# fp16 parts of x, q and k split with tokens in the partitions and turned by transposing DMAs, in an attention and FFN block on one core

## What is computed

```python
def ref(x, Wq, Wkv, Wout, bout, w_gate, w_up, w_down):
    xn = layernorm(x)
    # attention, 16 heads of 16; k and v are the same matrix
    q, kv = rotary(xn @ Wq), rotary(xn @ Wkv)
    att = softmax(q * 16 ** -0.5 @ kv.T)          # per head
    a = (att @ kv) @ Wout + bout
    # FFN, integer weights times 1/127, 768 hidden
    h = silu(xn @ wg.T) * (xn @ wu.T)
    return x + a + h @ wd.T
```

## Time and profile before

| | us |
|---|---|
| median of 3 runs | 850.45 |
| the profiled execution | 852.67 |
| its span | 850.9 |
| busy: TensorE, VectorE, ScalarE, GpSimd | 819.2, 758.6, 687.8, 213.3 |
| granted TensorE clock, mean over the span | 0.996 |

### The profile page before, as it was taken

The page is one execution under the profiler, slowest core; times in us unless marked ns, Lnnn a source line. Parts: engine busy times, 40 slices in busy tenths (PEclk is TensorE's granted clock), DMA queues, the critical chain, the costliest instruction groups (busy, mean ns, idle before and its releaser), DMA issues.

```text
span 850.9 us, 19487 instructions
## 1 busy us (share of the span) xinstructions
PE 819.2 (96%) x7500; PEld 316.0 (37%) x7500; DVE 758.6 (89%) x937; ACT 687.8 (81%) x1275; POOL 213.3 (25%) x458
## 2 busy tenths in 40 slices
PE   4898999999999999999999999999999999999997
PEld 2455555565433333333333333333333333333234
DVE  5897788888799999999999999999999999999802
ACT  4555354443699999999999999999999999999982
POOL 3623354334302100000222222222222222222210
PEclk9999999999999999999999999999999999999999
DMA  9212100111211111111221222122212121122222
GB/s 300 73 50 78 60 25 28 49 50 53 64 28 34 31 29 33 45 29 33 52 54 48 54 55 59 48 49 58 54 50 55 52 60 50 50 56 56 80 65 80
DMA packets 63615, 48.49 MB, mean 57 GB/s; under 512 B 23308, under 2 KB 53836, under 8 KB 63524
## 3 DMA queue, kind: packets, MB, share of 16 engines
q1 hardware_dynamic: 63524, 47.26, 20.0%
HBM read 28.57 MB, written 16.90 MB: 53 GB/s over the span
## 4 chain that ended last, share of the span: by engine, by line
PE 89%; ACT 3%; DVE 3%; issue 2%; POOL 0%; DVEq 0%; ACTq 0%
PE ps L740 33%; PE ps L757 18%; PE ps L722 14%; PE ps L600 8%; PE ps L628 4%; ACT arena L994 3%; PE ps L577 1%; PE ps L579 1%; PE ps L578 1%; PE ps L617 1%; PE ps L660 1%; PE ps L768 1%; PE ps L552 1%; DVE side L1094 1%; PE ps L784 1%
## 5 line engine op out<-in xcount | busy, mean ns | idle before, releaser
L1153 DVE TENSOR_REDUCE negmax<-ps 128x2 f32<-128x1024 f32 x512 | 588.9, 1211 | 8.6 <-PE ps L757 6.4
L994 ACT ACTIVATE arena<-ps 128x512 f32<-128x512 f32 x1024 | 555.5, 595 | 32.2 <-PE ps L722 10.5
L740 PE MATMUL ps<-arena 128*32 128x256 f32 x4072 | 326.5, 392 | 2.4 <-issue 2.2
L722 PE MATMUL ps<-qs,ks 51*128 51x512 f16 x1024 | 197.9, 382 | 3.4 <-ACT arena L994 2.2
L757 PE MATMUL ps<-ks,qs 48*128 48x512 f16 x972 | 189.4, 386 | 0.0
L740 PEld LDWEIGHTS ps<-arena 128*32 128x32 f32 x4072 | 80.4, 107 | 128.1 <-issue 127.0
L757 PEld LDWEIGHTS ps<-ks,qs 48*128 48x128 f16 x972 | 46.5, 92 | 195.1 <-DVE negmax L1153 136.1
L924 ACT ACTIVATE side<-ps 128x512 f32<-128x512 f32 x48 | 28.6, 597 | 90.6 <-PE ps L600 90.1
L600 PE MATMUL ps<-arena,side 128*128 128x512 f16 x384 | 91.3, 386 | 1.1 <-DVE side L1094 1.0
L722 PEld LDWEIGHTS ps<-qs,ks 51*128 51x128 f16 x1024 | 50.7, 93 | 78.1 <-ACT arena L994 46.1
L1399 POOL TENSOR_TENSOR arena<-arena,x_all 128x256 f32<-128x256 f32 x22 | 16.1, 732 | 229.6 <-ACT arena L1015 229.6
(11 more groups left out here) (116 smaller groups left out, 558.8 us busy)
## 6 DMA issues: line engine op xcount, KB each, us to landing
parts_d<-arena SPq DMA_DIRECT2D x64, 128.0 KB
x_all<-x_dram SPq DMA_DIRECT2D x8, 512.0 KB, 9.3
qs<-parts_d SPq DMA_DIRECT2D x64, 64.0 KB, 1.9
ks<-parts_d SPq DMA_DIRECT2D x64, 64.0 KB, 1.9
o_d<-arena SPq DMA_DIRECT2D x124, 32.0 KB
arena<-o_d SPq DMA_DIRECT2D x24, 128.0 KB
arena<-inv_d SPq DMA_DIRECT2D x48, 64.0 KB
out_dram<-arena SPq DMA_DIRECT2D x24, 128.0 KB, 1.8
```

Source lines behind the costliest of these rows:

```text
L722: mm = pe.matmul(ps[:, score_bank(place(p, kt, 2 * half + a)), :], ks[ring][top:top + ROWS, kt * P:(kt + 1) * P], qs[ring][top:top + ROWS, ...
L740: mm = pe.matmul(ps[32 * j:32 * j + 32, 7, cols], vstage[pl % 2][:, j % 2, kt, :], probs[PER_STEP * (kt % PBUF) + j][:, cols], start=(kt = ...
L994: act.activation(probs[PER_STEP * (kt % PBUF) + j], ps[:, score_bank(place(p, kt, j)), :], ACT.Exp).then_inc(exp_done, 1)
L1153: dve.tensor_reduce(negmax[pl % 2][:, h, :, kt], ps[:, bank:bank + 2, :], AX.X, ALU.max, negate=True).then_inc(max_done, 1)
```

## The change

What is split and turned, and by whom:

- x (chunks 1 to 7): ScalarE writes the high part `x_hi` from `xn` in SBUF, all 1024 columns in one operation; VectorE the low part `x_lo` = `xn` - `x_hi`, also in one, ahead of the first reduce of the chunk. Both have tokens in the partitions. SP turns each into `xh` and `xl` with one transposing DMA of 8 blocks. Chunk 0 is turned as before.
- q and k (all chunks): ScalarE writes `qk_hi` from `qk` in SBUF per token tile, ahead of the chunk's own silu; GpSimd writes `qk_lo` per token tile (`low_qk`, four subtractions of 512 columns, ahead of `keep_values`; in chunk 0 between its low parts of the hidden values). SP turns each with one transposing DMA of 16 blocks, waits until both have landed, and stores as before.
- TensorE has no `turn_x` (but chunk 0's) and no `turn_qk`; the waits on their banks go. The last chunk's down waits for the hidden values' parts alone.
- SP's order is, per chunk: turn x of c + 1, turn q and k of c, store c. The pair loads stand behind the second chunk's stores as before, the turn of the row maxima ahead of the last chunk's turns.
- VectorE: no `low_qk`; `low_w` moved between products 3 and 4 and behind 4 of chunk 0; twelve moments behind chunk 0's last product; `inverse` moved into `rope_chunk`.
- ScalarE waits for the last chunk's turns ahead of the first exponential, as the new tiles lie where the probabilities go.

The core of the diff:

```diff
@@ sync @@
 def store_chunk(b, s):
     c = b * CPB + s
+    sp.wait_ge(qk_turned, 32 * (c + 1))
     for g in range(4):
-        sp.wait_ge(lo_done, 4 * c + g + 1)
         for k in range(NPART):
             ...
+def turn_qk(c):
+    if c:
+        for g in range(4):
+            sp.wait_ge(parts_stored[g], 16 * NPART * c)
+    sp.wait_ge(qk_hi_done, CT * (c + 1))
+    sp.dma_start_transpose(parts[:, 0, :, :].rearrange("p g (t n) -> p (g t) n", t=CT),
+                           qk_hi.rearrange("p g t n -> p (g t n)")).then_inc(qk_turned, 16)
+    sp.wait_ge(qk_lo_done, CT * (c + 1))
+    sp.dma_start_transpose(parts[:, 1, :, :].rearrange("p g (t n) -> p (g t) n", t=CT),
+                           qk_lo.rearrange("p g t n -> p (g t n)")).then_inc(qk_turned, 16)
+def turn_x(c):
+    if c >= 2:
+        sp.wait_ge(up_done, KH * (c - 1))
+    sp.wait_ge(x_hi_done, c)
+    sp.dma_start_transpose(xh[c % 2].rearrange("p k (t n) -> p (k t) n", t=CT),
+                           x_hi.rearrange("p k t n -> p (k t n)")).then_inc(x_turned, 16)
+    sp.wait_ge(x_lo_done, c)
+    sp.dma_start_transpose(xl[c % 2].rearrange("p k (t n) -> p (k t) n", t=CT),
+                           x_lo.rearrange("p k t n -> p (k t n)")).then_inc(x_turned, 16)
...
@@ tensor @@
 def project(c):
-    pe.wait_ge(xT_copied, x_copies(c, KD - 1))
     if c:
-        pe.wait_ge(xl_ready, KD * (c + 1))
+        pe.wait_ge(x_turned, 32 * c)
+    else:
+        pe.wait_ge(xT_copied, 2 * KD)
...
     gate_up(c, 0)
     gate_up(c, 1)
-    if c + 1 < NCHUNK:
-        turn_x(c + 1)
...
-    if units[UNITS:]:
-        lead(units[UNITS])
-    turn_qk(c)
-    for n in units[UNITS + 1:]:
+    for n in units[UNITS:]:
         lead(n)
@@ scalar @@
 for c in range(NCHUNK):
     more = c + 1 < NCHUNK
-    if c:
-        high_qk(c - 1)
     if more:
         normalise(c + 1)
+        high_x(c + 1)
+    if c:
+        high_qk(c)
     silu(c, 0)
     silu(c, 1)
+    if c == 0:
+        high_qk(0)
     high(c, 0)
-    if more:
-        copy_x(c + 1, 0)
-        if c:
-            copy_x(c + 1, 1)
@@ vector @@
+def low_x(c):
+    if c == 1:
+        dve.wait_ge(wud_ready, 1)
+    else:
+        dve.wait_ge(x_turned, 32 * (c - 1))
+    dve.wait_ge(x_hi_done, c)
+    dve.tensor_tensor(x_lo.rearrange("p k t n -> p t k n"), xn.rearrange("p t (k n) -> p t k n", k=KD),
+                      x_hi.rearrange("p k t n -> p t k n"), ALU.subtract).then_inc(x_lo_done, 1)
...
     for j in range(2, KH):
         if c + 1 < NCHUNK and j == 2:
-            low_x(c + 1, 0)
+            low_x(c + 1)
...
@@ gpsimd @@
+def low_qk(c, t):
+    ...
+    pool.wait_ge(qk_hi_done, CT * c + t + 1)
+    pool.tensor_tensor(qk_lo[:, :, t, :], qk[:, t, :].rearrange("p (g n) -> p g n", g=4), qk_hi[:, :, t, :],
+                       ALU.subtract).then_inc(qk_lo_done, 1)
```

More of the change, by code:

```diff
@@ L160, in build @@
         front_room = used[0]
-        parts = [carve(NPART * CHUNK // 2, FP16, "p (s n) -> p s n", s=NPART) for _ in range(4)]
+        parts = carve(4 * NPART * CHUNK // 2, FP16, "p (s g n) -> p s g n", s=NPART, g=4)
         atile_hi = [carve(HG * P // 2, FP16, "p (g n) -> p g n", g=HG) for _ in range(2)]
@@ L462, in _ @@
                     sp.dma_start(ks[i][top:top + MPARTS, :], unit_rows[:, :]).then_inc(units_in, 16)
[L463 to L468, removed]
+            for c in range(NCHUNK):
+                if c + 1 < NCHUNK:
+                    turn_x(c + 1)
+                else:
                     turn_rows(0, 0)
                     load_mrows(0, 0)
+                turn_qk(c)
                 store_chunk(c // CPB, c % CPB)
+                if c + 1 == CPB:
+                    for p in range(2):
+                        load_pair(p, p)
             def load_last(g, landed):
@@ L603, in gate_up @@
                     mm.then_inc(done, 1)
[L605 to L618, removed]
             def down(c, t):
@@ L932, in high_qk @@
             def high_qk(c):
[L933 to L938, removed]
+                if c:
+                    act.wait_ge(qk_turned, 32 * c)
+                for t in range(CT):
+                    act.wait_ge(rope_done, CT * c + t + 1)
+                    act.activation(qk_hi[:, :, t, :], qk[:, t, :].rearrange("p (g n) -> p g n", g=4), ACT.Copy
+                                   ).then_inc(qk_hi_done, 1)
             roots(0, CT)
@@ L1067, in rotated @@
                 if t == 0:
[L1068 removed]
+                    dve.wait_ge(qk_hi_done, CT * c)
+                    dve.wait_ge(qk_lo_done, CT * c)
                     dve.wait_ge(v_kept, c)
@@ L1095, in gated @@
                                          ALU.mult, ALU.mult).then_inc(hid_done, 1)
-            def low_qk(c):
-                for g in range(4):
-                    dve.wait_ge(hi_done, 4 * c + g + 1)
-                    dve.tensor_tensor(parts[g][:, 1, :], bank_turn(g), parts[g][:, 0, :], ALU.subtract
-                                      ).then_inc(lo_done, 1)
             def add_ffn(c, t):
@@ L1115, in rope_chunk @@
                         rotated(c, t - 1)
+                    if c in (1, 2) and t == 1:
+                        inverse(c + 1, 2 * CT + 3 * CT * (c - 1), 2 * CT + 3 * CT * c)
                 rotated(c, CT - 1)
@@ L1352, in _ @@
                     split_max(0, 0)
+                if c:
+                    for t in range(CT):
+                        low_qk(c, t)
                 keep_values(c)
@@ L1355, in _ @@
                     low_hid(c, j)
+                    if c == 0 and 1 <= j <= CT:
+                        low_qk(0, j - 1)
             def stage_values(p, batch, slot, pair):
```

140 lines of the change are left out of this document (73 added, 67 removed).

## The result

The changed kernel takes 841.1 us (median of 4 runs, 840.25 to 842.6) where the kernel before, on the same chip, takes 849.88: ratio 0.9894, interval 0.9871 to 0.9917. The steps of the forecast added up to 1.2 us less; 8 to 9 came.

The account below looks back on a forecast made before the run. The prediction took TensorE as the bound, with VectorE second by tenths of a microsecond. Terms of -2.0 (chunks 0 to 2), +2.3 (chunks 3 to 6) and -1.5 (chunk 7) summed to -1.2 us: 849.3 us, no difference, range 842 to 864.

Parts of the forecast that it names:

- Removed from TensorE, steady chunks: Chunks 3 to 6: 2.6 us of turns leave TensorE per chunk, yet chunks grow 0.55 to 0.6, +2.3 us in all.
- The 2.6 us are gone twice over: Steady chunks: TensorE waits 2 us for the first reduce and 1 us at the end for silu and product.
- The transposing DMAs: SP queue: each further block costs 0.18 us, so turns hold SP 2.4 us (x) and 3.8 us (q and k).
- the idle TensorE ahead of it grows from 2.7 us to about 4.5: Chunk 2: TensorE's wait ahead of the first lead matmul lengthens, that matmul coming at 82.6 us.
- I keep that loss: Chunk 2: the stretch of lower clock (0.72 of full in 80 to 92 us) was assumed to remain.
- partly fill gaps: Chunk 0: weights' low parts moved between products on VectorE partly fill gaps; products end at 37.1, -2.5 us.
- I leave 1.1 of the 2.5: Chunk 1: of chunk 0's 2.5 us gain 1.1 stays; low x ready at 56.4, chunk 2 starts at 64.3.
- ScalarE's copies stay equal in number of columns: ScalarE's splitting copies, with GpSimd's new subtractions, were costed at nothing.
- Chunk 7: Last chunk: down no longer waits for low parts and starts right behind the last lead, -1.5 us.
- A: Rival: SP becomes the bound if a block costs over 0.33 us; 862 us at 0.37, 967 at 0.72; chance 0.15.
- C: Rival: TensorE's waits in chunks 3 to 6 lower its clock, +13.6 us, 863 us; chance 0.1.
- B: Rival: low x cheaper or not locked out, 846.3 us; wholly covered, chunks of 23.8 and 842 us; chance 0.2.

Follow-up runs that it names:

- e6: Changed kernel with TensorE turning the identity matrix, unread, where it had turned x and q and k: 845.15 us, ratio 0.9942.
- e2: Changed kernel with the next chunk's low part of x made among the rotations (chunk 1: ahead of the first gated product): 834.41 us, ratio 0.9826.
- e5: The kernel before, unchanged, profiled a second time: 848.19 us.
- e1: Changed kernel with SP's first pair loads held back until the first gate group of chunk 2 is done: 844.92 us, ratio 0.9951.
- e7: Changed kernel with each transposing DMA cut in two, 8 and 4 blocks instead of 16 and 8: 842.53 us, ratio 0.9907.
- e8: Changed kernel with the low parts of q and k on VectorE instead of GpSimd, both inputs in SBUF: 849.77 us, ratio 0.9999.
- e4: Changed kernel with weights' low parts, moments and inverses put back where the kernel before has them: 847.01 us, ratio 0.9974.
- e9: Changed kernel with low part of x among the rotations and, in chunks 2 to 6, lead pairs and reduces one place later: 833.17 us, ratio 0.9798.
- e10: Changed kernel with the low part of x among the rotations, run again for comparison on one chip: 835.04 us, ratio 0.9820.
- e11: The changed kernel again, unchanged, for comparison on one chip: 841.52 us, ratio 0.9903.

## Why the prediction was wrong

**Removed from TensorE, steady chunks: right in mechanism.** "The 2.6 us are gone twice over" holds: the rows in chunk 4 name the low part of x, the reduce and the last product, e6 gives the turns back for 0.65 us, and e2 shows what paces the chunks. The size was off: +0.1 to +0.2 in each of chunks 3, 4 and 6 where +0.55 stood. The wait of "0.73" was 0.69; the operation itself took 1.21 instead of 1.27 and low x ended 0.2 us sooner, and the handovers behind it took 8.7 us instead of 8.85. In chunk 5 the forecast added 0.6 to a period of 25.86, but that chunk's extra 0.7 came from the collision in the earlier trace rows, and the collision is gone: `combine` never took over 178 ns in the changed kernel. Together 2.4 of the missing 5.9 us.

**The transposing DMAs: the mis-sized term that cost most.** "A turn of x holds SP 2.4 us, one of q and k 3.8": measured 1.2 and 1.8 to 2.3. With it the sum from low x to the end of the stores, 16.2 us in the forecast, was 13.1 (54.17 to 67.27). The other half is the start of that sum: low x at 56.4 forecast, 54.1 measured. Of the 3.1 us the hold alone gave 4.5: the three transposes ahead of the stores took 5.6 us of SP, gaps included, where 10.1 stood. The landing took 1.5 back, 2.7 us from the end of the last one's hold to the first store (59.76 to 62.42) where 1.2 stood. So stores ended 5.3 us before the forecast's 72.6, and "first lead 82.6" became 76.08. It could not have come earlier: it is TensorE's own arrival. The step that failed is "the idle TensorE ahead of it grows from 2.7 us to about 4.5"; it vanished, and "I keep that loss" of the clock did not hold in the profiled execution either. Chunk 2 became 24.6 us long, against 27.5 in e5 and 31.4 in the execution that the forecast worked from, of which it took off 0.9. e1 puts the idle time back and pays 3.3 us at the next mark.

**Chunk 0: -2.5 forecast, -3.8 measured.** VectorE, the kernel before again (e5), then the changed one:

```profile
35.11 0.69 DVE L1094 SCALAR_TENSOR_TENSOR side<-ps,side 128x512 f32<-128x512 f32 x1 [0.67 <-ACT side L924]
35.72 2.94 DVE L1086 SCALAR_TENSOR_TENSOR arena<-wqkv,wgain,arena 128x512 f16<-128x512 f32 x2
```
```profile
31.73 1.06 DVE L1113 SCALAR_TENSOR_TENSOR arena<-wqkv,wgain,arena 128x512 f16<-128x512 f32 x1
32.85 0.69 DVE L1121 SCALAR_TENSOR_TENSOR side<-ps,side 128x512 f32<-128x512 f32 x1
33.46 0.90 DVE L1113 SCALAR_TENSOR_TENSOR arena<-wqkv,wgain,arena 128x512 f16<-128x512 f32 x1
34.58 0.69 DVE L1121 SCALAR_TENSOR_TENSOR side<-ps,side 128x512 f32<-128x512 f32 x1 [0.21 <-PE ps L626]
```

The low parts "partly fill gaps" was too timid: at their new place they take 1.96 us instead of 2.94 and none of it is on the path, because six moments that stood there (2 x 1.26) had moved behind the last product, under the projection. The projection starts at 35.41 against 39.19. (In chunk 0 single executions stray: the 35.41 of the changed kernel is 36.64 in e7, with 1.2 us of it older than anything that e7 changes.)

**Chunk 1: "I leave 1.1 of the 2.5".** 2.65 of 3.8 were left. The moments cost what they should (35.18 to 39.99, 4.8 us ahead of the rotation), against 5.8 in e5 (38.58 to 44.36: six moments, the inverse with its wait for ScalarE, low q and k). And low x, made whole, no longer stands between the fourth and fifth product: 0.6 us more. What took the rest back is a term that the forecast put at nothing ("ScalarE's copies stay equal in number of columns"): their place. VectorE's rotations start 4.4 us earlier than in e5, but the chunk's first silu starts at 50.81 against 50.67. ScalarE now has ahead of it the norm (at 44.19, behind the moved `inverse`), the high part of x and those of q and k of this same chunk, until 49.49, and then a table load of 1.28 us, which in e5 lay at 45.35. TensorE waits for the products behind that silu:

```profile
52.27 3.61 PE L626 MATMUL ps<-arena,side 128*128 128x512 f16 x16 [2.33 <-DVE side L1121]
```

No run moves these copies, so what they cost is read from the rows and not tested.

**Chunk 7: right.** -1.45 for -1.5, and the wait it names is gone: the last lead starts at 212.54 after 1.65 us for its reduce, down at 212.93.

**The rivals.** A (SP the bound) is out: at most 0.11 us a block, by the longest hold (1.91 us for 8), where 0.33 were needed, and e7. C (the clock) is out in the steady chunks: waits of 1.64 and 0.93 us left it at full in every profiled execution. B's number is the nearest to the result (842), but its mechanism is not what the changed kernel did: low x was locked out and uncovered. e2 covers it, and there B's figure of 23.8 for covered chunks was right (23.6).

The Trainium skill's rule on the pair of ports (SBUF — State Buffer, SBUF: two separate sides) is borne out in both directions: VectorE, the later one at 126.75, takes 0.69 us longer beside GpSimd's first (from 126.42, 1.16 long alone, so until 127.58, 0.83 us behind VectorE's start), and GpSimd's second then waits for VectorE (3.24 us for its two, 2.31 where nothing is beside them). That is a lock for a whole instruction, and in e8, where VectorE came first, VectorE waited for nothing. Its entry of 1309 ns for a 128x128 by DMA (VectorE: DVE Perf Modes, The three transpose paths) is near SP's time for a DMA of one block (1.14 us) and of eight (1.23 at the least), and does not multiply with the blocks.

What stays open: the execution of before with the low clock is explained as far as its longer wait (2.72 against 1.30 us) goes, but not why its loads took 1.6 us longer to release the lead matmul. Nor is it known what of the difference of the medians is the clock's.

## What to carry to other kernels

A DMA's hold on the queue and its transfer are two terms; price them apart, and when both bounds of one are far apart, run the sum at each and look for a wait that vanishes at one end: there the outcome jumps. A load issued early in a pipeline can be worth more than the engine time that the change is about: holding it back cost 3.3 us here, the 2.6 us of turns given back to TensorE 0.65 a steady chunk. One profiled execution can hold a stretch of low clock that the next does not; look at a second before a stage is priced. When the work that covered a late engine is taken away, find what was late behind it, and move that too: here 1.7 us in each steady chunk waited for one line's place.

## What the runs showed of the hardware

- Transposing DMAs, SBUF to SBUF, fp16 blocks of 128x128: SP held 1.14 us for 1 block (the median), and at the least 1.19 for 4, 1.23 for 8, 1.32 for 16 (2.26 to 2.58 for one right behind another of 16); landing after 2.3, 2.4, 3.2 and 4.4 us at the least.
- Low parts on VectorE, float32 less fp16, both in SBUF: 1024 columns 1.21 us, four of 512 columns 3.33, or 0.83 each, against 0.62 each from PSUM (four in 2.48).
- The granted clock fell to its lower level, half of full, in stretches of 3.4 us (6.8 once). In the front of the thirteen profiled executions, from some 17 us on, where the record of the clock begins, it did so nine times, each time just behind an idle TensorE: 2.02 us idle (e4, at 66.6), 2.08 (e9), 2.33 (e7), 2.55 (e1), 2.72 (before), 2.73 (e10), 3.05 and 3.99 (e8), 4.08 (e4). The same idle times also left it at full: 2.33 in the changed kernel, e1 and e11, 2.43 in e5, 2.72 in e2. So the length of a wait alone does not say whether the clock falls; no fall came behind an idle time under 2 us.
